# A gated cross-attention and 2:4-sparse feed-forward kernel: token validity folded into the softmax, mask loads split, and work reordered in the attention and in the first pair

## The reference

```python
scores = einsum('bsd,bmd->bsm', layernorm(x), ctx) / sqrt(512)
scores = where(mask[:, None, :], scores, -1e30)
attn = softmax(scores);  readout = einsum('bsm,bmd->bsd', attn, ctx)
readout = where(any(mask, -1)[:, None, None], readout, 0)
x = x + tanh(g_xattn) * readout
h = silu(layernorm(x) @ w_gate) * (layernorm(x) @ w_up)     # inner width 2048
h = keep the 2 of each 4 neighbours with the largest magnitude, others 0
x = x + tanh(g_ffn) * (h @ w_down)
```

## Time and profile before

| | us |
|---|---|
| median of 3 runs (lowest, highest) | 1117.73 (1117.38, 1119.66) |
| the profiled execution, its own time | 1116.94 |
| its span, first to last instruction | 1115.1 |
| PE busy | 1082.4 (97%) |
| DVE busy | 809.6 (73%) |
| ACT busy | 620.1 (56%) |
| POOL busy | 210.6 (19%) |
| attention, until PE's first product | 134.58 |
| first pair, PE from unit 2 on | 173.8 |

### The profile page before, as it was taken

One profiled execution on the slowest core, in us unless ns is written; L12 is line 12 of the kernel. 1 busy time (PEld: TensorE's weight loads), 2 busy tenths in 40 slices (PEclk: granted clock), 3 DMA queues, 4 the chain that ended last, 5 costly groups with the idle time before them and its releaser, 6 DMA issues.

```text
span 1115.1 us, 15146 instructions
## 1 busy us (share of the span) xinstructions
PE 1082.4 (97%) x4960; PEld 880.0 (79%) x4960; DVE 809.6 (73%) x1400; ACT 620.1 (56%) x1132; POOL 210.6 (19%) x328
## 2 busy tenths in 40 slices
PE   6998799999999999999999999999999999999998
PEld 5776587777878888888888888888888888888886
DVE  6999969879897757576775767675757565565765
ACT  5999678566765544454544444454445454443452
POOL 5576610121210111111111111001111111111111
PEclk9999999999999999999999999999999999999999
DMA  7899586798869977797779777888878666767726
GB/s 273 295 349 329 202 326 226 219 289 280 257 226 354 356 196 198 187 257 185 202 197 374 182 202 200 237 235 208 231 230 274 151 153 156 189 159 189 199 29 137
DMA packets 89533, 254.75 MB, mean 228 GB/s; under 512 B 9072, under 2 KB 9072, under 8 KB 85104
## 3 DMA queue, kind: packets, MB, share of 16 engines
q1 hardware_dynamic: 67856, 205.55, 52.2%
q0 software_dynamic: 21600, 48.24, 26.1%
HBM read 154.14 MB, written 99.61 MB: 228 GB/s over the span
## 4 chain that ended last, share of the span: by engine, by line
PE 73%; DVE 14%; ACT 4%; issue 4%; POOL 2%; DMA 2%; SPq 0%; DVEq 0%; ACTq 0%; POOLq 0%
PE ps_y L1302 9%; PE ps_a L1231 9%; PE ps_a L1233 9%; PE ps_a L1235 9%; PE ps_y L1304 9%; PE ps_y L1303 9%; PE ps_d L1233 4%; PE ps_d L1231 4%; PE ps_d L1235 4%; PE ps_c L1233 2%; PE ps_c L1231 2%; PE ps_c L1235 2%; DVE beats L980 2%; DMA w_raw<-in_L_ffn_w_up 1%; DVE x1n L930 1%
## 5 line engine op out<-in xcount | busy, mean ns | idle before, releaser
L569 POOL DMA_DIRECT2D out_rows<-y_out x124 | 107.1, 871 | 735.2 <-ACT y_out L717 712.7
L1231 PE MATMUL ps_a<-xm,w_ring 128*128 128x512 f32 x512 | 200.7, 392 | 3.6 <-ACT cp L597 3.3
L1233 PE MATMUL ps_a<-xm,w_ring 128*128 128x512 f32 x512 | 200.3, 391 | 0.0
L1235 PE MATMUL ps_a<-xm,w_ring 128*128 128x512 f32 x512 | 200.2, 391 | 0.0
L1302 PE MATMUL ps_y<-dn,h_hi 128*128 128x512 f32 x480 | 188.9, 394 | 4.4 <-ACT y_out L717 3.3
L1304 PE MATMUL ps_y<-dn,h_lo 128*128 128x512 f32 x480 | 187.4, 390 | 0.0
L1303 PE MATMUL ps_y<-dn,h_hi 128*128 128x512 f32 x480 | 187.0, 390 | 0.0
L717 ACT ACTIVATE y_out<-ps_y,ffn_gate 128x512 f32<-128x512 f32 x124 | 84.8, 686 | 158.4 <-PE ps_y L1304 158.3
L694 ACT ACTIVATE h_hi<-hidden 128x512 fp32r<-128x512 f32 x128 | 73.6, 626 | 107.0 <-DVE hidden L1006 107.0
L980 DVE TENSOR_TENSOR beats<-h_abs 128x512 bf16<-128x512 f32 x186 | 117.7, 684 | 1.3 <-ACT h_abs L687 1.3
L1231 PEld LDWEIGHTS ps_a<-xm,w_ring 128*128 128x128 f32 x512 | 96.4, 188 | 26.2 <-issue 5.2
(11 more groups left out here) (109 smaller groups left out, 1876.6 us busy)
## 6 DMA issues: line engine op xcount, KB each, us to landing
w_ring<-w_scratch SPq DMA_DIRECT2D x147, 512.0 KB, 4.5
out_rows<-y_out POOLq DMA_DIRECT2D x124, 256.0 KB, 4.3
w_scratch<-w_ring SPq DMA_DIRECT2D x56, 512.0 KB, 4.7
xm_scratch<-x_out SPq DMA_DIRECT2D x42, 512.0 KB, 5.4
xm<-xm_scratch SPq DMA_DIRECT2D x21, 1024.0 KB, 8.4
w_raw<-in_L_ffn_w_down SPq DMA_DIRECT2D x9, 1024.0 KB, 7.8
x_in<-in_x SPq DMA_DIRECT2D x32, 256.0 KB, 4.7
ctx_in<-in_ctx SPq DMA_DIRECT2D x32, 256.0 KB, 5.0
```

Source lines behind the costliest of these rows:

```text
L569: nc.gpsimd.dma_start(out[RING * (n // (2 * TILES * QS)) + TILES * ORDER[order] + n % TILES], y_out[:, n % 4], accum_op=ALU.add).then_inc( ...
L1231: nc.tensor.matmul(to, w_ring[:, k, e, 0, c], xm[:, k, 0, c], start=begins and c == 0, stop=False, skip_group_check=not begins)
L1233: nc.tensor.matmul(to, w_ring[:, k, e, 0, c], xm[:, k, 1, c], start=False, stop=False, skip_group_check=not begins)
L1235: last = nc.tensor.matmul(to, w_ring[:, k, e, 1, c], xm[:, k, 0, c], start=False, stop=c == 1, skip_group_check=not begins)
```

## The change

- The scores get one more column, 0.9e30 (`FEW`), that only the row minimum sees. A row with no valid token then has exponentials and a sum of 0, and 1e-30 (`LEAST`) is added to each sum before the power. `valid`, `gate_valid` and their waits go; `probsT` is scaled by the gate alone.
- POOL's sum before the power now covers the softmax sum too, so it waits for the exponential already there; and POOL waits for DVE's `x1n` of the slot before it converts the mask or makes low parts.
- The mask is loaded and converted in four parts, in slots 1, 5, 7 and 10; the gates are loaded after x of b = 2; the first two weight pieces go ahead of x of b = 7.
- The tables of spreads, sums, low parts and pieces change.
- In the first pair: on ACT the token factors of point 3 of step 0, point 0 of step 1 and point 1 of steps 1 to 3 stand behind the first copies; in odd units the spreads stand earlier against the absolutes and the third behind `silu1`. On DVE the low parts of dn stand ahead of the last two compares in steps 2 to 4, and token low parts move with their high parts.

```diff
+FEW = 0.9e30
+LEAST = 1e-30
-CONVERT = {1: (0,), 2: (1,), 3: (2, 3)}
+CONVERT = {1: 0, 5: 1, 7: 2, 10: 3}
-PIECE_AT = {4: (0, 2), 7: (0, 3), 10: (1, 0), 13: (1, 1), 21: (1, 2), 24: (1, 3), 27: (2, 0), 30: (2, 1)}
-SPREAD_AT = {3: (0, 0), 6: (0, 1), 9: (0, 2), 12: (0, 3), 20: (1, 0), 23: (1, 1), 26: (1, 2), 29: (1, 3)}
-SUM_AT = {13: ((0, 0), (0, 1)), 14: ((0, 2),), 15: ((0, 3),), 30: ((1, 0), (1, 1))}
-W0_AT = {5: 0, 8: 1, 14: 2, 15: 3, 16: 4, 17: 5, 18: 6}
-X0_AT = {19 + i: (0, i) for i in range(7)} | {29 + i: (1, i) for i in range(7)}
+PIECE_AT = {6: (0, 2), 7: (0, 3), 10: (1, 0), 11: (1, 1), 20: (1, 2), 21: (1, 3), 36: (2, 0), 37: (2, 1)}
+SPREAD_AT = {5: (0, 0), 6: (0, 1), 8: (0, 2), 9: (0, 3), 19: (1, 0), 20: (1, 1), 35: (1, 2), 36: (1, 3)}
+SUM_AT = {11: (0, 0), 12: (0, 1), 13: (0, 2), 14: (0, 3), 37: (1, 0), 38: (1, 1)}
+W0_AT = {7: 0, 10: 1, 14: 2, 15: 3, 16: 4, 17: 5, 18: 6}
+X0_AT = {21 + i: (0, i) for i in range(7)} | {28 + i: (1, i) for i in range(7)}
...
             for b in range(INPUTS):
                 load(b)
-                if b == 1:
-                    sp.dma_start(mask_in, mask.rearrange("b m -> (b m)").rearrange("(a n) -> a n", a=1)
-                                 .to_broadcast([P, B * M])).then_inc(mask_loaded, 16)
+                if b == 6:
+                    load_w_piece(sp, nc.sync, 0, 0)
+                    load_w_piece(sp, nc.sync, 0, 1)
+                if b == 7:
+                    load_mask(1)
+                if b == 2:
+                    load_mask(0)
...
-            load_w_piece(sp, nc.sync, 0, 0)
-            load_w_piece(sp, nc.sync, 0, 1)
+            load_mask(2)
+            load_mask(3)
...
-                if first or second:
-                    part_v = slice(0 if first else 1, 2 if second else 1)
-                    nc.gpsimd.tensor_tensor(base3[:, k, part_v], bn_mv[:, k, part_v, 1], eps[:, part_v],
-                                            ALU.add).then_inc(base_done, 1)
-                    pool.wait_ge(base_done, n + 2)
+                part_p = slice(0 if first else 1, 3 if third else 2 if second else 1)
                 if third:
                     pool.wait_ge(probs_done, n - 3)
-                part_p = slice(0 if first else 1, 3 if third else 2 if second else 1)
+                nc.gpsimd.tensor_tensor(base3[:, k, part_p], stats[:, k, part_p, 1], least[:, part_p],
+                                        ALU.add).then_inc(base_done, 1)
+                pool.wait_ge(base_done, n + 2)
...
+                if second:
+                    pool.wait_ge(x1n_done, n - 5)
                 if n in CONVERT:
...
-                if n in CONVERT:
-                    dve.wait_ge(mask_loaded, 16)
-                    for m in CONVERT[n]:
-                        nc.vector.tensor_reduce(valid[:, m * RING:(m + 1) * RING],
...
-                if n + 1 in X0_AT:
-                    x_sum(dve, 0, *X0_AT[n + 1])
+                if n in X0_AT:
+                    x_sum(dve, 0, *X0_AT[n])
...
-                if n == 3:
-                    dve.wait_ge(valid_done, 4)
-                    dve.wait_ge(gates_done, 1)
-                    nc.vector.tensor_scalar(gate_valid[:], valid[:], xattn_gate[:], None, ALU.mult).then_inc(gate_valid_done, 1)
...
                     copy_a0(u, 1)
+                    if s == 1:
+                        x_high_at(0, 3)
...
-                    x_high_at(s, 0)
+                    if s > 1:
+                        x_high_at(s, 0)
                     copy_d0(u, 0)
                     copy_d0(u, 1)
+                    if s == 1:
+                        x_high_at(s, 0)
...
-                    x_high_at(s, 1)
+                    if s >= QS:
+                        x_high_at(s, 1)
...
                     w_high(act, 2, 6)
-                    x_high_at(0, 3)
                     continue
...
                 copy_a0(u, 1)
+                if s < QS:
+                    x_high_at(s, 1)
                 for j in tiles[2:]:
                     h_high(s - 1, 1, j)
+                if building:
+                    spread(act, u + 1, 0)
                 for j in first:
                     absolute(s, 0, j)
                 silu0(u, 0)
                 silu0(u, 1)
+                if building:
+                    spread(act, u + 1, 1)
                 copy_a1(u, 0)
...
                 x_high_at(s, 2)
-                if building:
-                    spread(act, u + 1, 0)
                 copy_d0(u, 0)
-                if building:
-                    spread(act, u + 1, 1)
                 copy_d0(u, 1)
                 if building:
                     w_high(act, u + 1, 0)
-                    spread(act, u + 1, 2)
                 silu1(u, 0)
                 silu1(u, 1)
                 if building:
+                    spread(act, u + 1, 2)
                     w_high(act, u + 1, 1)
...
-                    x_low_at(s, 0)
+                    if s > QS:
+                        x_low_at(s, 0)
                     add_c22(u, 0)
                     add_c22(u, 1)
+                    if s <= QS:
+                        dn_low(s - 1)
+                        x_low_at(s, 0)
                     compare(s - 1, 1, REST[2:])
-                    if s - 1 in DN_BUILT:
+                    if s > QS and s - 1 in DN_BUILT:
                         dn_low(s - 1)
...
                     add_c11(2, 1)
+                    x_low_at(0, 3)
                     count_wins(0, 0)
                     keep(0, 0, kept_order(0))
-                    x_low_at(0, 3)
...
                 add_c11(u, 1)
+                if s < QS:
+                    x_low_at(s, 1)
```

More of the change, by code:

```diff
@@ L163, in flamingo_gated @@
         neg_mean_rstd = sb("neg_mean_rstd", [P, RING], F32, 4)
-        eps = sb("eps", [P, 2], F32, 4)
+        least = sb("least", [P, 3], F32, 4)
         minus_one = sb("minus_one", [P, 1], F32, 4)
@@ L167, in flamingo_gated @@
         gates_in = sb("gates_in", [P, 2], F32, 4)
-        valid = sb("valid", [P, B], F32, 4)
-        gate_valid = sb("gate_valid", [P, B], F32, 4)
         ident = sb("ident", [P, P], F32, 4)
@@ L202, in flamingo_gated @@
         ctx_in_loaded = [sem(f"ctx_in_loaded{k}") for k in range(INPUTS)]
-        gates_loaded, mask_loaded, mask_neg_done = sem("gates_loaded"), sem("mask_loaded"), sem("mask_neg_done")
+        gates_loaded, mask_neg_done = sem("gates_loaded"), sem("mask_neg_done")
+        mask_loaded = [sem(f"mask_loaded{k}") for k in range(B // RING)]
         neg_mean_done, shift_done = sem("neg_mean_done"), sem("shift_done")
-        base_set = sem("base_set")
+        stats_set, few_set = sem("stats_set"), sem("few_set")
         ident_set, ident_done, half_done = sem("ident_set"), sem("ident_done"), sem("half_done")
-        gates_done, valid_done, gate_valid_done = sem("gates_done"), sem("valid_done"), sem("gate_valid_done")
+        gates_done = sem("gates_done")
         bn1_done, stats1_done, bn2_done, stats2_done = (
@@ L506, in _ @@
         def _(pool):
-            nc.gpsimd.memset(base3[:], 1.0).then_inc(base_set, 1)
-            nc.gpsimd.memset(eps[:], EPS)
+            nc.gpsimd.memset(ident[:], 0.0).then_inc(ident_set, 1)
+            nc.gpsimd.memset(stats[:], 1.0).then_inc(stats_set, 1)
+            nc.gpsimd.memset(least[:, 0:2], EPS)
+            nc.gpsimd.memset(least[:, 2:3], LEAST)
             nc.gpsimd.memset(minus_one[:], -1.0)
-            nc.gpsimd.memset(exponent3[:], -0.5).then_inc(half_done, 1)
-            pool.wait_ge(half_done, 1)
+            nc.gpsimd.memset(exponent3[:, 0:2], -0.5)
             nc.gpsimd.memset(exponent3[:, 2:3], -1.0).then_inc(half_done, 1)
-            nc.gpsimd.memset(ident[:], 0.0).then_inc(ident_set, 1)
+            nc.gpsimd.memset(neg_scores[:, :, M:M + 1], FEW).then_inc(few_set, 1)
             pool.wait_ge(ident_set, 1)
@@ L914, in _ @@
                 if n in SUM_AT:
-                    for u, i in SUM_AT[n]:
-                        w_sum(dve, u, i)
-                if n + 1 in X0_AT:
-                    x_sum(dve, 0, *X0_AT[n + 1])
+                    w_sum(dve, *SUM_AT[n])
+                if n in X0_AT:
+                    x_sum(dve, 0, *X0_AT[n])
                 b = n - 5
@@ L929, in _ @@
                     dve.wait_ge(power_done, n + 2)
-                    nc.vector.tensor_scalar(x1n[:, b % 2], x1[:, b % 4], bn_mv[:, n % RING, 1, 0:1],
+                    nc.vector.tensor_scalar(x1n[:, b % 2], x1[:, b % 4], stats[:, n % RING, 1, 0:1],
                                             power3[:, n % RING, 1:2], ALU.subtract, ALU.mult).then_inc(x1n_done, 1)
```

53 lines of the change are left out of this document (29 added, 24 removed).

## The result

The changed kernel takes 1106.91 us (median of 4, 1106.67 to 1108.09); the kernel before, on the same chip, 1118.35 (4 runs, 1117.38 to 1119.66). The ratio is 0.9896, with a 95% interval of 0.9882 to 0.9909, so 11.4 us are won. The prediction was 1101.1 with a range of 1095.5 to 1107.5: the direction holds, and the range by 0.6 us at its slow end, but 16.6 us were forecast. The profiled executions differ by 10.2 us (1116.94 and 1106.78), and their spans by 10.5 (1115.1 and 1104.6); I explain the spans.

What follows compares the result with a forecast made beforehand. Attention was taken as bound by a POOL-DVE loop, the first pair by DVE, and PE as full past 345 us. 1116.94 - 13.4 - 3.2 = 1100.3, median 0.79 higher: 1101.1; range 1095.5 to 1107.5.

Steps and rivals of the forecast that it cites:

- both parts: Attention: 13.4 us won, bounds 9 and 15; first feed-forward pair: 3.2 us won, bounds 0 and 8.
- rivals 1 and 2: Rival 1: pair gives nothing, 1104.3, 18%; rival 2: attention gives only 9, low part meeting DVE sums, 1105.5, 15%.
- the prediction's own signs: Right: PE's first product at 121.2 +- 1.5; wrong: slots above 3.4 in 16 to 23 (POOL late).
- The pair as far as unit 4: Units 2, 3 and down(0,1): net 0 in unit 2, +0.5 and -1.0 in unit 3, +2.1 at down(0,1), balance +1.6.
- pieces (2,0) and (2,1): Rival 5, unit 0: these pieces, loaded in slots 36 and 37, hold up ACT and every copy; 1120, 2%.
- The range's ends: Low: rival 3 with a high attention (15 + 7: 1095.5); high: rivals 1 and 2 (9 + 1: 1107.7).
- To slot 11: Attention's start: earlier b = 2 and no `valid` reductions, less spreads two in a row; 4.6 us won, bounds 3.2 and 5.6.
- 21 to 29: Attention slots 21 to 29: 34.63 us becomes 30.87, five slots of 3.27 and four of 3.63; 3.8 won.
- The sums beside POOL: Slots 31 to 34: a DVE sum may meet POOL's low part, up to 0.9 us for each of four returns.
- Past 345 it is kept, for PE is full there: After the first pair: the pair's 3.2 us gain stays, PE being busy 742.00 of 742.00 us from 345 on.
- The half clock: Unit 2, PE's stop before k = 5: the clock should fall again, costed at nothing, 1.7 us if not.

Runs made afterwards that it cites:

- the four other kernels with this attention: Changed kernel with old pair order (1108.63 us), DVE's old step 4 order (1106.06), `x_blk` load sooner (1108.64), or those last two together (1105.64).
- the last kernel: Changed kernel plus sums behind `x1`, earlier `x_blk`, `dn_low` behind second compare, two pieces and two `w_high` later, spread behind `copy_a1` (units 3, 5): 1100.75 us.
- the attention alone: The changed attention, tables and first loads, with the pair's ACT and DVE order of the kernel before: 1108.63 us, ratio 0.9902.
- the wait alone: The kernel before plus only POOL's wait for `x1n` before mask conversion or low parts: 1113.01 us, ratio 0.9946.

## Why the prediction was right in direction and range, and 5 us too hopeful

**What held.** The range held, but narrowly and with some luck: both parts came out 3 us short (10.0 of 13.4, 0.5 of 3.2), and the result is that of rivals 1 and 2 together more than that of the forecast, by other causes than theirs. The mechanism of the attention held: POOL's low part under `x1n` cost 0.9 us a slot, the wait takes it away, and the spacing becomes 3.27 in plain slots and 3.63 to 3.66 in those with a sum. The wait made POOL late nowhere between 16 and 30. Two of the prediction's own signs failed all the same: the first product came at 124.57 and not within 1.5 of 121.2, and slots 20 and 21 took 3.48 and 3.47, above its 3.4. There POOL's base waited for DVE (1.93 and 1.65 us) and DVE once for the scores (0.28), and ACT, with spreads in slots 19 and 20, was busy 16.00 of 16.00 us from 62 to 78; the prediction costed two spreads in a row for the slots to 11 and not here. That is read from the trace, no run tests it. The pair as far as unit 4, step by step, relative to the first product: k = 2 of unit 2 2.1 sooner; a stop of 3.5 before k = 5, net 0.02 (forecast 0); k = 2 of unit 3 0.53 sooner (0.5); k = 4 0.57 late (0.5); no stop at down(0,1), unit 4 1.49 sooner (1.6). Units 5 and 6 gave 0.4 less than costed, down(2,0) 2.48 instead of 3.2. Nothing waited for pieces (2,0) and (2,1). (The range's ends don't follow from their sums by 0.2 us: 1117.73 less 22 is 1095.7, less 10 is 1107.7. It changes nothing.)

**"To slot 11", 4.6, measured 2.6.** In the profile of the changed kernel ACT has no idle time from 21.7 us on, and its exponential holds POOL's base of slot 11 by 0.94. In the four other kernels with this attention the power of slot 11 comes 0.5 to 1.6 us sooner though nothing was changed there, and some 0.4 of that is gone again by slot 12. So the gain to slot 11 is 2.6 to 4.2 over five profiles, and to slot 12 (45.58 before, 41.84 to 42.97 in the five) 2.6 to 3.7; it is 4.6 in none. One cost was missing in all of them: POOL waits for the first part of the mask, whose conversion it starts at 20.6 here; slot 5 takes 3.54. In the kernels with an earlier start that slot takes up to 4.43, so the order of the first loads limits this part; no run changed it, and what is left of the 2 us is open.

**"21 to 29", 3.8, measured 2.8.** The step took the slots' length from DVE and POOL alone. x comes late in slot 25, 4.18 instead of 3.64, with the DMA engines busy all the time (share 1.03 from 62 to 94 us); slot 21, above, and slot 23 (3.38 here, 3.67 to 4.15 in the four others with this attention) are most of the rest. The prediction counted the moved pieces as a risk of their own lateness, never as loads in the way of x. The run with two pieces later shows it.

**The sums beside POOL.** In slots 13 and 14 the forecast 3.63 became 3.89; slot 30 took 3.56 instead of 3.2, slots 31 to 33 3.41 instead of 3.25. The prediction looked for such a meeting, but in the wrong shape: a DVE sum made longer by POOL's large low part, 0.9 for each. It weighed the Trainium skill's "SBUF — State Buffer", "SBUF: two separate sides", for that. What happened is the reverse: no sum of the attention is longer than 0.73 in any of these kernels, 0.68 or 0.69 in nearly all, and POOL's small operations wait, 0.57 and 0.48 us. Two things in the Trainium skill's section agree with the rows: that these two contend, and that whoever starts first keeps the other out, as far as the sum comes first. A base or `neg_mean` that starts inside a sum ends 0.05 us after the sum does, wherever it started. The other way round it doesn't show: 58 powers in these traces start 0.07 to 0.11 us before a sum, and neither is longer for it, 0.85 or 0.70 and 0.68. (The long power of slot 13 is recorded 0.02 ahead of its sum, 46.66 and 46.68; POOL's spans are rough, and this is too close to tell who was first.) In size this is the 2.0 us that the sums behind `x1` brought, scatter of the start included.

**"Past 345 it is kept, for PE is full there": the step that failed**, worth 2.1 us. PE was full there, but with what slack? The copies of step 4 hang on two loads: `x_blk`, which SP issues behind 7 MB of `xm`, and `dn_raw`, which POOL issues 12 us later (356.10). Before, `x_high` there had waited 2.64 us already without stopping PE: a warning that a full engine doesn't give. In the new order it waits 3.11, and the change itself put `dn_low` ahead of two compares in this step, so the late load went straight into the `keep` that `copy_y` needs. Both had to be mended to get the 1.9 us. The size of 2.1 is partly luck: the same step cost up to 4.5 in other kernels with this order.

**The half clock** in unit 2 was costed at nothing, 1.7 if not. It came (0.68 and 0.63 us for a matmul above) and put PE 1.47 us behind at k = 6, and at unit 3's k = 2 nothing of it was left. The run with `x_blk` sooner had no low clock after the same stop and reached k = 2 at the same relative time, to 0.01. So nothing was the right price here, but a narrow one: in the last kernel the low clock lasted longer, PE was 2.32 behind, and 0.65 of it reached unit 3.

## What to carry to other kernels

Read the slack of a stage that "is full" before you call a gain kept: look for the loads and copies in it that already wait without stopping the bound engine, since work that arrives sooner meets loads that don't. When a loop is made faster, add up the bytes of the slots too: the pace may be right for every engine and still ask for more than the DMA engines gave (here 378 to 391 GB/s), and a load that nobody needs for a dozen slots is the first to move. Where two engines must meet, move the meeting onto an instruction that nobody waits for. And before a difference between two single profiles is called the effect of an edit, look at the same place in the other kernels in which that stage is the same: slot 10 above took 4.19 in one of five and 3.3 or 3.4 in the others.

## What the runs showed of the hardware that I had not expected

- A sum of DVE with both inputs in SBUF (128x512, 0.68 us) holds up small operations of POOL that start inside it until it ends: base 0.19 to 0.67, `neg_mean` 0.19 to 0.58 us, and power 0.85 to 1.34 or 1.42 in 13 of 14 meetings in which the two start within 0.06 us of each other. The sum keeps its 0.68, and a power that starts 0.07 us or more before it keeps its 0.85. So a shift of 0.1 us decides over 0.5. A `x1n` of DVE with one such input is itself lengthened, 0.55 to 1.44, by POOL's low part of 1.27.
- The same stop of PE is not always followed by the same clock. Before k = 5 of unit 2 PE stood for 3.52, 3.47 and 3.51 us in three kernels; the granted clock over the next 5 us was 0.66, 1.00 and 0.50:

```profile
182.00:187.00 5.00, 4.98 (x15) 3.99 (x16) 5.00 (x9) 4.13 (x6) 1.29 (x2) 0.66 0.11 30
```

```profile
181.40:186.40 5.00, 4.92 (x21) 3.85 (x22) 5.00 (x9) 4.16 (x6) 1.26 (x2) 1.00 0.10 34
```

```profile
178.50:183.50 5.00, 4.95 (x12) 3.92 (x13) 5.00 (x9) 4.18 (x6) 1.24 (x2) 0.50 0.12 34
```

  (the changed kernel, the one with `x_blk` sooner, and the last one). Shorter stops went both ways as well: after 1.91 us before k = 2 of unit 2 the clock fell in the kernel before (0.66 over 5 us) and stayed at 1.00 in the kernels with the attention alone and with the wait alone. The Trainium skill, "TensorE: Matmul & The Clock Gate", "HAM oscillation — how this bites in real kernels", blames idle gaps of PE; the rows agree in kind, but a single gap's length doesn't tell.
- Such a stretch at 1.2 GHz costs 1.5 to 1.6 us where PE is the bound (down(0,1) with the attention alone and with the wait alone, step 4 with `x_blk` sooner, the first products without the wait), and nothing where PE waits for DVE next.
- A load of 1 MB behind seven others of 1 MB lands at no fixed time: ACT waited for `x_blk` 2.6 to 6.8 us in the eight kernels that load it there. Issued at 344 us in the changed kernel it was used first at 366.5; issued at 339.6, ahead of two of the seven `xm`, it held nobody at 362.8.
